# Sharing of P's PSUM banks by the x and y transposes, a third bank for the MLP's hidden pieces, and the MLP's second product one tile a step

## The reference

```python
x = x + roll_back(window_attention(roll(layernorm(x))))   # windows of 8 x 8, 12 heads of 16
x = x + gelu(layernorm(x) @ fc1_w + fc1_b) @ fc2_w + fc2_b # 192 -> 768 -> 192, exact gelu
```

## Time and profile before

| | |
|---|---|
| median of 3 runs (lowest to highest) | 4231.57 us (4228.81 to 4232.9) |
| span of the profiled execution | 4229.7 us |
| busy: PE, DVE, ACT, POOL | 92%, 81%, 64%, 73% |
| granted clock of PE (mean) | 0.999 of full speed |
| transfers | DMA engines busy about half the time, 100 GB/s |

### The profile page before, as it was taken

One profiled execution on the slowest core, in us unless ns is written; L12 is line 12 of the kernel. 1 busy time (PEld: TensorE's weight loads), 2 busy tenths in 40 slices (PEclk: granted clock), 3 DMA queues, 4 the chain that ended last, 5 costly groups with the idle time before them and its releaser, 6 DMA issues. The chain is left out here.

```text
span 4229.7 us, 174430 instructions
## 1 busy us (share of the span) xinstructions
PE 3910.8 (92%) x65872; PEld 2873.4 (68%) x65872; DVE 3431.5 (81%) x9093; ACT 2718.6 (64%) x5921; POOL 3089.0 (73%) x6257
## 2 busy tenths in 40 slices
PE   3999999999999999999999999999999999999998
PEld 2667667766766776676676677667667766666765
DVE  6888888888888888888888888888888888888885
ACT  1666666666666666666666666666666666666665
POOL 4777777777777777777777777777777777777774
PEclk9999999999999999999999999999999999999999
DMA  4644545545554454555546455455544545554543
GB/s 101 109 92 103 102 98 100 103 101 97 104 101 97 103 103 98 102 100 103 97 102 103 98 100 105 100 99 103 104 94 104 101 98 101 100 105 95 95 98 62
DMA packets 1545149, 421.03 MB, mean 100 GB/s; under 512 B 1441782, under 2 KB 1542522, under 8 KB 1544316
## 3 DMA queue, kind: packets, MB, share of 16 engines
q1 hardware_dynamic: 1540732, 409.87, 49.6%
q10 hardware_dynamic: 3584, 0.01, 0.0%
HBM read 32.15 MB, written 25.17 MB: 14 GB/s over the span
## 5 line engine op out<-in xcount | busy, mean ns | idle before, releaser
L964 DVE TENSOR_TENSOR hid<-scaled,hid 128x512 f16<-128x512 f32 x768 | 677.7, 895 | 348.2 <-POOL hid L1133 328.1
L594 PE MATMUL bank<-w_fc,hid 128*128 128x192 f16 x9216 | 846.1, 246 | 106.1 <-DVE hid L964 104.7
L581 PE MATMUL ps_s<-xh,w_fc 128*128 128x512 f16 x3840 | 866.6, 379 | 70.6 <-ACT stage L705 67.8
L1070 POOL TENSOR_TENSOR rstd<-vare,half 128x2 f32<-128x2 f32 x520 | 361.3, 695 | 766.8 <-DVE vare L904 766.7
L594 PEld LDWEIGHTS bank<-w_fc,hid 128*128 128x128 f16 x9216 | 761.9, 98 | 195.0 <-DVE v_blk L920 169.6
L581 PEld LDWEIGHTS ps_s<-xh,w_fc 128*128 128x128 f16 x3840 | 355.8, 97 | 567.3 <-issue 109.6
L1133 POOL TENSOR_SCALAR hid<-scaled 128x512 f16<-128x512 f32 x768 | 562.9, 738 | 130.6 <-ACT scaled L719 129.2
L719 ACT ACTIVATE scaled<-ps_s,b_fc 128x512 f32<-128x512 f32 x768 | 529.5, 690 | 155.2 <-PE ps_s L581 121.0
L684 ACT ACTIVATE xs<-xn 128x192 f16<-128x192 f32 x512 | 184.8, 361 | 664.3 <-POOL xn L1077 664.3
L711 ACT ACTIVATE pt<-ps_t 128x768 f16<-128x768 f32 x512 | 415.3, 811 | 304.4 <-PE ps_t L538 301.4
L457 PE MATMUL bank<-w_qkv,xh 128*128 128x384 f16 x2560 | 501.8, 326 | 6.2 <-DMA xh<-xs 3.6
(11 more groups left out here) (113 smaller groups left out, 7192.9 us busy)
## 6 DMA issues: line engine op xcount, KB each, us to landing
x_img<-in_x_dram SPq DMA_DIRECT2D x256, 96.0 KB, 2.2
out_dram<-y_img SPq DMA_DIRECT2D x256, 96.0 KB, 2.0
xh<-xs SPq DMA_TRANSPOSE x520, 2.5
qkt<-qk SPq DMA_TRANSPOSE x512, 3.3
ot<-os SPq DMA_TRANSPOSE x512, 2.3
stage<-in_L_conv_fc_w_dram SPq DMA_DIRECT2D x2, 384.0 KB, 4.3
stage<-in_L_conv_w_fc_dram SPq DMA_DIRECT2D x2, 384.0 KB, 4.2
stage<-in_L_conv_qkv_w_dram SPq DMA_DIRECT2D x2, 288.0 KB
```

What stands on the lines that cost most here:

```text
L581: last = mm(ps_s[:, u % 2, :].rearrange("p (a t) -> p a t", a=GROUP), w_fc1[layer][:, part, m * 128:(m + 1) * 128], xh[:, p % 2 * GROUP:(p ...
L594: mm(bank[:, 0:C], hid16[:, hs, m, tok], w_fc2[layer][:, ws, m, :], start=(m == 0 and i == 0), stop=False)
L964: v.tensor_tensor(hid16[:, 1, m, :], hid[:, u % 4, :], hid16[:, 0, m, :], ALU.subtract)\
```

## The change

The bank `ps_tr` is given up for transposes. x's transposes go to P's first bank (`ps_x`), y's to P's second (`ps_y`), both between `p_lo` of one tile and the transpose of P of the next; the freed bank (`ps_hid`) takes hidden pieces 0 and 5. Pieces 1 to 4 use the two score banks in turn, so only piece 1 waits for the exp. Four pieces are still issued in q0 but behind a second product. `mlp_out` runs one tile a step, in q1, q2, q3 and the next q0; the tile of q1 uses `ps_o`, the others `ps_v`. On ACT the gelus 2 to 5 stand together at the start of q1, gelu 0 moves behind `qk_hi`, and the x and y evacuations move ahead of `norm2_hi`. On DVE all six `hidden_lo` stand in q1, `mlp_residual` moves from the end of a step to the head of the next, and in q1 `p_lo` moves ahead of `v_lo`. In q2 PE's V product goes ahead of P times V, whose wait is now for the residual of tile 0.

```diff
-        ps_tr, ps_o, ps_qk, ps_v = banks
+        ps_hid, ps_o, ps_qk, ps_v = banks
+        hid_banks = [ps_hid[:, :], ps_s[:, 0, :], ps_s[:, 1, :], ps_s[:, 0, :], ps_s[:, 1, :], ps_hid[:, :]]
+        ps_x = ps_t[:, 0, 0:C]
+        ps_y = ps_t[0:H2, 1, 0:2 * TOK].rearrange("p (k t) -> p k t", k=2)
...
                 def x_transpose(n):
-                    take_tr("x_in", rank(n))
+                    ge("p_lo", min(n - 8, ENDS))
+                    ge("x_in", rank(n) - 1)
...
                 def v_product(n):
-                    if place == 1 or p < 0 or p == 0 == place:
+                    if n < LATE + 2 or place == 2:
                         ge("v_lo", n - 1)
                     else:
-                        ge("resid2", p * GROUP + (-1, None, 0, 2)[place])
+                        ge("resid2", n - LATE - 2)
...
                 def p_transpose(n):
                     ge("p_lo", n - 1)
+                    if live(s + 6) and visit(s + 6)[1] == 0:
+                        ge("x_in", rank(s + 6))
+                    if live(s - LATE - 3) and visit(s - LATE - 3)[1] == 1:
+                        ge("y_ready", rank(s - LATE - 3))
...
                 def pv_product(n):
-                    if mlp and place == 3:
-                        ge("resid2", p * GROUP + 1)
+                    if mlp and place == 2:
+                        ge("resid2", p * GROUP)
...
                 if live(s + 3):
                     qk_product(s + 3)
+                if live(s - LATE - 1):
+                    mlp_out(s - LATE - 1, ps_o if place == 1 else ps_v)
                 if mlp and place == 0:
-                    for m in range(3):
+                    for m in range(4):
                         hidden(m)
...
@@ vector
+                if live(s - LATE - 2):
+                    mlp_residual(s - LATE - 2, ps_o if place == 2 else ps_v)
                 if mlp and place == 1:
-                    hidden_lo(2)
-                    hidden_lo(3)
+                    for m in range(4):
+                        hidden_lo(m)
                 if live(s + 5):
                     mean_variance(s + 5, 0)
-                if live(s - 2):
-                    inverse_sums(s - 2)
                 if mlp and place == 1:
                     hidden_lo(4)
                 if live(s - 2):
+                    inverse_sums(s - 2)
                     o_norm(s - 2)
                 if live(s):
                     row_max(s)
                 if live(s - 3):
                     attention_residual(s - 3)
-                    statistics(s - 3, 1)
-                if live(s):
-                    v_lo(s)
                 if mlp and place == 1:
                     hidden_lo(5)
+                    if live(s - 1):
+                        p_lo(s - 1)
+                    if live(s):
+                        v_lo(s)
+                if live(s - 3):
+                    statistics(s - 3, 1)
...
-                if mlp and place > 0:
-                    mlp_residual(p * GROUP + (0, 0, 2, 3)[place], ps_v)
```

More of the change, by code:

```diff
@@ L400, in slot @@
                     load(visit(s + 9)[0] + 1, visit(s + 9)[2])
[L401 to L404, removed]
+                n = s - LATE - 5
+                if live(n) and visit(n)[1] == 1:
+                    ge("y_ready", rank(n) | 1)
+                    store(visit(n)[0], visit(n)[2])
             run(slot)
@@ L499, in rel_scores @@
                     if place == 1:
-                        ge("gelu", p * HC + HC - 1)
+                        ge("gelu", p * HC + 4)
                     ge("exp_done", n - 1)
@@ L590, in mlp_out @@
                     if n % GROUP == 0:
-                        ge("h_lo", p * HC + HC - 1)
+                        ge("h_lo", n // GROUP * HC + HC - 1)
+                        ge("o_norm", min(s - 2, ENDS))
+                    else:
+                        ge("v_lo", min(s, ENDS))
+                        ge("resid2", n - 1)
                     for m in range(HC):
@@ L598, in y_transpose @@
                 def y_transpose(n):
-                    take_tr("y_ready", rank(n))
+                    ge("p_lo", min(s - 2, ENDS))
+                    ge("y_ready", rank(n) - 1)
                     ge("resid2", n)
                     for k in range(2):
-                        last = nc.tensor.transpose(ps_tr[0:H2, k * TOK:(k + 1) * TOK], token_rows(n)[:, k * H2:(k + 1) * H2],
+                        last = nc.tensor.transpose(ps_y[:, k], token_rows(n)[:, k * H2:(k + 1) * H2],
                                                    ident[:, :])
@@ L627, in slot @@
                     p_transpose(s - 1)
-                if place == 1 and live(s - LATE - 2) and visit(s - LATE - 2)[1] == 1:
-                    y_transpose(s - LATE - 2)
-                if mlp and place == 2:
-                    if visit(p * GROUP)[1] == 1:
-                        y_transpose(p * GROUP)
-                    ge("o_norm", min(s - 2, ENDS))
-                    mlp_out(p * GROUP + 1, ps_o)
-                if mlp and place == 3 and visit(p * GROUP)[1] == 1:
-                    y_transpose(p * GROUP + 2)
                 if live(s):
@@ L678, in x_evac @@
                     ge("xtr", rank(n))
-                    copy(stream(n, 0), ps_tr[:, 0:C], ACT.Copy).then_inc(S["x_in"], 1)
+                    copy(stream(n, 0), ps_x, ACT.Copy).then_inc(S["x_in"], 1)
                 def norm2_hi(n):
@@ L718, in gelu @@
                     ge("h_lo", u - 4)
-                    nc.scalar.activation(hid[:, u % 4, :], ps_s[:, u % 2, :], ACT.Gelu, bias=b_fc1[layer][:, m:m + 1],
+                    nc.scalar.activation(hid[:, u % 4, :], hid_banks[m], ACT.Gelu, bias=b_fc1[layer][:, m:m + 1],
                                          scale=UNSCALE).then_inc(S["gelu"], 1)
@@ L738, in y_evac @@
                             act.wait_ge(y_stored[h], 16 * image)
-                    tile = ps_tr[0:H2, 0:2 * TOK].rearrange("p (k t) -> p k t", k=2)
-                    for win, img in box_pairs(t, tile, y_img[:, :, :]):
+                    for win, img in box_pairs(t, ps_y, y_img[:, :, :]):
                         last = copy(img, win, ACT.Copy)
@@ L772, in slot @@
                     load_gelu()
-                    gelu(0)
                 if live(s + 3):
@@ L776, in slot @@
                 if mlp and place == 0:
+                    gelu(0)
                     gelu(1)
-                if last_block and place == 2:
-                    y_evac(p * GROUP + 1)
             run(slot)
@@ L1141, in slot @@
                     hidden_hi(4)
+                    hidden_hi(5)
                 if live(s - 4):
@@ L1145, in slot @@
                     set_mask(s + 3)
-                if mlp and place == 1:
-                    hidden_hi(5)
                 if live(s - 2):
```

68 lines of the change are left out of this document (24 added, 44 removed).

## The result

The changed kernel takes 4323.97 us (median, 4320.01 to 4331.9) against 4230.98 us of the kernel before on the same chip: 1.0219 times as long, 95% interval 1.0207 to 1.0231. It is slower, as forecast, and 29 us slower than the 4295 forecast, inside the range. The profiled execution took 4326.28 us. All times compared here are of fast executions; of e6 and e9 only a slow one was profiled, so nothing is read from their traces.

The account below looks back on a forecast made before the run. PE, busy 92%, was taken as the bound, with DVE's in-order list about as full. Terms summed to +0.55 us a group in B and +0.48 in A; mean +0.52 times 127 is +65 on 4229.7: 4295, range 4240 to 4355.

Parts of the forecast that it names:

- P times V in q2: PE waits there for tile 0's residual from DVE: 1.4 us in L1 groups, 0.6 in L0, over 100 in all.
- The V products of q3 and q0: P times V in q2 to q3's V product 6.45 or 6.5 us, then 6.0 to q0's; each follows DVE's residual by 0.15.
- next h - V0: From the V product of the next q0 to the next first hidden product: 4.85 us in place of 3.86, +0.99.
- P2 - H: From the hidden products' end to P times V in q2: 8.52 us in B (+1.03), 8.62 in A (+0.74).
- B: The group with attention of L1: 31.88 us before, forecast 32.43, +0.55.
- H: Mark in a group: end of the hidden products; forecast put the fifth low half 1.3 us after it, tile 0's residual 8.0.
- The second chain: ACT's table load, norm2_hi, v_hi and copy of P, then DVE's list, put tile 0's residual at H + 7.9.
- Of the old waits the one for the row maximum stays: PE's 0.7 us wait for the row maximum in q1 stays, as DVE's list up to it is no shorter.
- A: The group with attention of L0: 32.19 us before, forecast 32.67, +0.48.
- Head and tail: Time of the span outside the repeating groups: a change of 5 us either way allowed.
- Full gain: Rival: tile 0's residual comes before PE needs it, all three waits go, some 215 us: 4015; chance 0.06.
- Slower still: Rival: low halves 4 and 5 collide in full with POOL's norm work, residual 0.78 later: about 4395; chance 0.09.

Follow-up runs that it names:

- e6: Changed kernel with POOL's high half of piece 4 ahead of norm1's low half in q1, and each MLP residual ahead of its step's closing statistics: 4227.2 us.
- e9: Kernel before, in q1: POOL's high halves of pieces 4, 5 ahead of norm1's, norm2's low halves; DVE's last low half and V's ahead of statistics: 4158.38 us.
- e4: Changed kernel with an extra, unread DVE reduction of 128 x 512 ahead of the sixth low half in q1: 4384.72 us.
- e3: Changed kernel with the old banks: x's and y's transposes have their own bank again, hidden pieces use the two score banks: 4330.87 us.
- e2: Changed kernel with POOL's high half of hidden piece 4 ahead of norm1's low half in q1: 4249.96 us.
- e1: Changed kernel with tile 0's residual on DVE right behind v_lo in q1, not at the head of q2: 4375.3 us.
- e10: Changed kernel with tile 0's second MLP product in the freed bank (ps_hid), so P times V shares no bank with it: 4300.38 us.
- e11: e10 and e2 together, on the changed kernel: 4218.63 us.
- e12: The kernel of e9 run once more, for a trace at full clock and a closer interval: 4154.02 us.

## Why the prediction was right, and where its size was off

*Direction and mechanism: right.* P times V in q2 waits for tile 0's residual, 1.34 us in the group shown (forecast 1.4), 126.6 us in all ("over 100"). The exp wait and the low half wait are gone. The V products of q3 and q0 fall within 0.2 of their terms, and next h - V0 is exact. That they follow DVE's residual by 0.15 is not so in both: they start 0.06 and 0.28 after its end. In q0 V's product stands 0.59 behind P times V, PE's own distance, so there the second of two nearly equal bounds held. e4 shows DVE's list on the path; e3 shows that the shared banks, priced at nothing, cost nearly nothing.

*The term that was mis-sized is P2 - H in B: 8.97 for 8.52.* Its first input was the fifth low half at H + 1.3, "it may come sooner". It came at H + 1.68 (2121.41 less 2119.73), beyond the upper end of 1.6, and at H + 1.58 in most other groups, which is where it was before. I had expected POOL's high half, 1.05 before, to be quicker beside a less busy DVE. It took 1.05 again, with the fourth low half (2119.87, 0.95) begun before it; the next high half, begun at 2121.27 before DVE's next, took 0.61. So the assumption that failed is that DVE would be out of its way. Nor had I read what stands ahead of it in POOL's list: the low half of norm1. It stood there before too, so it isn't what made the term wrong, but e2 takes it away and gains 74 us. From the fifth low half to the residual it then took 6.89, forecast 6.7; the sixth low half at 0.87 instead of 0.69 is most of it. PE's start behind the residual, 0.40 for 0.51, took back 0.11: 0.38 + 0.19 - 0.11 is the 0.45 within rounding. The second chain, over ACT, was not the tighter one: ACT's copy of P began at 2123.18 and DVE took it up at 2124.85, behind its own work.

*"Of the old waits the one for the row maximum stays": wrong in this group.* It was 0.71 and is 1.19, 118.6 us in all for 62.3. The reciprocal and the later fifth low half put the row maximum at H + 3.20, for H + 2.73 before (1500.06 less 1497.33). I had counted the reciprocal into the residual's time but not into this wait. It adds nothing to the sum, since the residual ends last; it moves part of the same lateness ahead.

*A group, forecast and measured.* Undisturbed ones average 32.58 against my 32.55, since A came out shorter (32.32 and 32.71, for 32.67) and B longer (32.65 for 32.43): 4 of the 29 us. That the two errors nearly cancel is luck. The larger part is something to which I gave no term: the groups that are not undisturbed. They exceed the others by 30 us in all, for 8 before, which makes 21. Of the 30, 19 are the new waits for the attention output's transfer, and some 8 are seven stretches at half clock (last section). Head and tail, allowed 5 either way and counted as none, add 3: the first hidden product is 0.4 later, and from the last group's first to the end it takes 26.1 us for 23.3.

*The rivals.* Full gain would have needed the residual by H + 5.7; it came at H + 8.57. "Slower still" named the right place, DVE and POOL in q1, but the residual was late by 0.57 (H + 8.57 for 8.0) and not by 0.78. Its mechanism is there, in part: an operation is lengthened when it starts beside or behind one of the other engine: a low half and a high half that both start at 2118.61 take 0.68 and 1.16; in e1 a high half from 2011.80 takes its 0.61 and the low half from 2011.94 takes 1.02 in place of 0.69. By the Trainium skill ("SBUF — State Buffer", section "SBUF: two separate sides") the one that starts second stands still while the other works. The first pair comes near that (1.16 is 0.55 over 0.61, for an overlap of 0.68), the second less so (0.33 for 0.47), as does the high half of piece 4 above (0.44 for 0.57). I had given that rule too little weight.

*What stays open.* Why the projection's input comes late in so many groups (1.8 us before, 19.1 changed, 71.3 in e10, 81.6 in e11). The less P times V waits in q2, the more the projection waits, mostly in q3 and q0 behind it; but the kernel before and e12, in which P times V doesn't wait for a residual at all, hardly have it. The median from issue to landing hardly moves (2.3 and 2.4 us). What grows is the time from POOL's end of the data to SyncE's issue: half of the transfers go within 0.35 us in each of these kernels, but one in ten needs over 0.67 before, 1.36 changed and 2.06 in e10. In a group of e10 with a wait of 1.89 us, SyncE's rows around it show the transposing transfers of three kinds, an image load and a store issued one behind the other, and the attention output's one only 2 us after its data. Whether the stores, which the change spreads over all steps, are what delays it was not tried.

## What to carry to other kernels

When a wait is moved, follow the late engine's list back to the first instruction that itself waited, and read what stands ahead of its producer: here half a microsecond of unurgent work on GpSimd cost 45 us in one kernel and 74 in the other, where all the bank moves together made 7. A bank of one's own gives back only part of a wait if the same engine is late for the next thing: 63 of 126.6 us in undisturbed groups. Read the groups that keep the clockwork's length apart from the others, since an edit can gain in the first and lose in the second. Before work is made earlier within an in-order list, check that its input is ready there, and who hangs on what it passes: the same residual was worth -25 us in one place and +51 four instructions ahead.

## What the chip showed that I had not expected

Behind a wait PE sometimes loses clock as well. In the changed kernel this happens seven times between the first group and the last six. Five times it is behind a wait of 1.4 to 1.8 us for the very residual that the change put in the way, twice behind one for the projection's input:

```profile
1273.21 0.75 PE L558 MATMUL bank<-v_blk,pt 128*64 128x34 f16 x36 [1.43 <-DVE x_tok L936]
...
1276.42 0.85 PE L526 MATMUL ps_s<-smax,neg_ident 128*128 128x384 bf16 x2
```

The shift of the scores takes 0.85 there and 0.50 elsewhere. The granted clock of that stretch (start and end, length, busy time of PE, of its loads, of DVE, ACT and POOL, then the clock, share of DMA, GB/s):

```profile
1274.23:1277.64 3.41, 3.41 (x23) 2.70 (x17) 3.02 (x10) 1.89 (x5) 3.03 (x9) 0.50 0.28 65
```

Half of full is the lower level of 1.2 GHz. Four of the five groups take 33.8 us for 32.65: 1.15 us for the clock. In e10 it happens six times, each time behind a wait for the transfer, here:

```profile
2297.65 0.86 PE L455 MATMUL bank<-w_proj,ot 128*128 128x192 f16 x5 [1.89 <-DMA ot<-os]
...
2299.75 0.85 PE L526 MATMUL ps_s<-smax,neg_ident 128*128 128x384 bf16 x2
```

```profile
2297.60:2300.00 2.40, 2.35 (x13) 2.19 (x14) 1.24 (x4) 0.01 (x1) 0.00 (x0) 0.54 0.84 192
2300.00:2302.00 2.00, 2.00 (x12) 1.20 (x11) 1.48 (x5) 1.98 (x3) 1.01 (x2) 0.70 0.60 129
2302.00:2304.00 2.00, 2.00 (x21) 1.56 (x19) 0.21 (x1) 1.75 (x4) 1.19 (x3) 1.00 0.70 165
```

Not every such wait does it. The 1.34 us ahead of P times V in the group shown did not, and neither did a longer one in the changed kernel:

```profile
404.94 0.57 PE L455 MATMUL bank<-w_proj,ot 128*128 128x192 f16 x5 [2.06 <-DMA ot<-os]
...
406.09 0.49 PE L526 MATMUL ps_s<-smax,neg_ident 128*128 128x384 bf16 x2
```

So a wait can cost its length and then a microsecond or more, and no run here shows which waits will. The kernel before and e12 have one such stretch each, in their last groups.
